# A routed FFN in which each half of a block takes its own expert

## The reference

```
# GNN, on the normalized x
h = layer_norm(x, gamma, beta)
conv = (adj @ h) @ W_rel + b_rel + h @ W_root
x = x0 + (x + relu(conv))            # x0 is the input, x its normalized form

# mixture of experts, on the normalized x
gate = x @ Wg.T + bg                 # 8 scores
topk_scores, topk_idx = top_k(gate, 2)
combine = softmax(topk_scores) placed at topk_idx
for e in range(8):
    h = relu(x @ W1[e].T + b1[e])    # 128 -> 512
    y = h @ W2[e].T + b2[e]          # 512 -> 128
    out = out + combine[e] * y
x = x + out
```

## Time and profile before

| what | us |
|---|---|
| median of 3 runs (479.68 to 481.05) | 480.88 |
| the profiled execution, its own time | 481.32 |
| its span, first to last instruction | 479.5 |
| PE matmuls busy | 393.0 (82%) |
| DVE busy | 315.6 (66%) |
| ACT busy | 271.5 (57%) |
| POOL busy | 249.9 (52%) |
| PE's share of the chain that ended last | 57% |

### The profile page before, as it was taken

The page is one execution under the profiler, slowest core; times in us unless marked ns, Lnnn a source line. Parts: engine busy times, 40 slices in busy tenths (PEclk is TensorE's granted clock), DMA queues, the critical chain, the costliest instruction groups (busy, mean ns, idle before and its releaser), DMA issues.

```text
span 479.5 us, 13216 instructions
## 1 busy us (share of the span) xinstructions
PE 393.0 (82%) x4371; PEld 350.2 (73%) x4371; DVE 315.6 (66%) x1055; ACT 271.5 (57%) x572; POOL 249.9 (52%) x263
## 2 busy tenths in 40 slices
PE   2888878789998679889867999999999999999000
PEld 2873735579997568889856988889999999998000
DVE  4875764685679497756898557765478545588511
ACT  1787583557885547786634686555555555554000
POOL 3002720177710377774007777777777750777770
PEclk9998785999999799999999999999999999999755
DMA  8991740164234234633436537647567857554520
GB/s 274 389 413 69 277 98 12 40 149 112 74 83 100 68 98 109 155 94 80 66 79 172 138 102 139 142 112 162 145 153 178 202 133 121 135 156 140 175 71 33
DMA packets 100721, 65.30 MB, mean 136 GB/s; under 512 B 66866, under 2 KB 92466, under 8 KB 100020
## 3 DMA queue, kind: packets, MB, share of 16 engines
q1 hardware_dynamic: 66292, 34.68, 27.4%
q0 software_dynamic: 8192, 16.79, 12.2%
q10 hardware_dynamic: 26176, 12.98, 11.1%
HBM read 19.58 MB, written 31.85 MB: 107 GB/s over the span
## 4 chain that ended last, share of the span: by engine, by line
PE 57%; DVE 22%; ACT 7%; issue 6%; DMA 3%; POOL 3%; ACTq 0%; SPq 0%; DVEq 0%; POOLq 0%
PE PY L951 7%; PE PY L946 7%; PE PY L947 7%; PE PH L927 6%; PE PH L929 6%; PE PH L928 6%; DVE HL L521 5%; POOL YG L307 3%; PE PY L938 2%; DVE STI L361 2%; PE PB L848 2%; PE PA L856 2%; PE PA L857 2%; ACT N L670 2%; DVE STO L407 1%
## 5 line engine op out<-in xcount | busy, mean ns | idle before, releaser
L294 POOL DMA_INDIRECT rows<-XHL,IDX x128 | 124.2, 970 | 136.0 <-DVE IDX L503 97.9
L521 DVE SCALAR_TENSOR_TENSOR HL<-PH,HH 128x512 f16<-128x512 f32 x198 | 129.9, 689 | 63.6 <-ACT HH L727 61.0
L307 POOL DMA_INDIRECT YG<-yrows,IDX x128 | 121.5, 949 | 81.7 <-DMA yrows<-YB 43.6
L727 ACT ACTIVATE HH<-PH 128x512 f16<-128x512 f32 x198 | 115.4, 594 | 29.4 <-PE PH L929 24.1
L947 PE MATMUL PY<-W2H,HL 128*128 x792 | 131.8, 220 | 0.0
L946 PE MATMUL PY<-W2H,HH 128*128 x792 | 131.8, 220 | 0.0
L927 PE MATMUL PH<-XT,W1H 128*128 128x256 f16 x396 | 108.1, 273 | 2.7 <-DVE HL L521 1.7
L951 PE MATMUL PY<-W2L,HH 128*128 x792 | 109.5, 220 | 0.0
L929 PE MATMUL PH<-XT,W1L 128*128 128x256 f16 x396 | 108.0, 273 | 0.0
L928 PE MATMUL PH<-XT,W1H 128*128 128x256 f16 x396 | 107.9, 273 | 0.0
L735 ACT ACTIVATE YB<-PY 128x256 f32<-128x256 f32 x99 | 37.9, 383 | 97.4 <-PE PY L951 92.3
(11 more groups left out here) (192 smaller groups left out, 504.8 us busy)
## 6 DMA issues: line engine op xcount, KB each, us to landing
yrows<-YB ACTq DMA_DIRECT2D x47, 256.0 KB
rows<-XT SPq DMA_DIRECT2D x2, 3072.0 KB, 16.3
YG<-in_w SPq DMA_DIRECT2D x2, 2048.0 KB, 11.3
out<-X SPq DMA_DIRECT2D x16, 256.0 KB
X<-in_x SPq DMA_DIRECT2D x3, 1024.0 KB, 5.5
ADJ<-in_adj SPq DMA_DIRECT2D x32, 64.0 KB
rows<-XHL,IDX POOLq DMA_INDIRECT x128
YG<-yrows,IDX POOLq DMA_INDIRECT x128, 2.5
```

Source lines behind the costliest of these rows:

```text
L294: nc.gpsimd.indirect_dma_start(rows[g % 2], bass.IndirectOffsetOnAxis(ap=IDX[:, col:col + 1], axis=0), XHL[:, src:src + 2 * P].bitcast(F32 ...
L307: nc.gpsimd.indirect_dma_start(YG[g % 2][:, dst:dst + P], None, yrows[g], bass.IndirectOffsetOnAxis(ap=IDX[:, col:col + 1], axis=0)).then_ ...
L521: nc.vector.scalar_tensor_tensor(HL[:, at:at + 2 * BW], PH[p % 2 * 2 + h][:, :], 0.0, HH[:, at:at + 2 * BW], ALU.max, ALU.subtract).then_i ...
L727: nc.scalar.activation(HH[:, at:at + 2 * BW], PH[p % 2 * 2 + h][:, :], ACT.Relu).then_inc((hia_made, hib_made)[h], 1)
```

## The change

The padding of the table goes to whole parts of 128 rows in place of 256. Two parts that follow one another form a block, and each has its own expert. A group then needs at most 2s + 7 parts, which is s + 4 blocks: 12, 20, 20, 20 and 12, in all 84.

- `expert(p)` becomes `experts(p)` and loads two registers.
- `hidden(p)` gets a loop over the two parts t: 24 matmuls of 128 columns, with the weights' address taken from the part's register, in place of 12 of 256 columns.
- `output(p)` works off the parts one after the other: each has its b2 matmul of 128 columns and 12 of the second layer. In all 26 matmuls of 128 columns in place of 24 and one of 256.
- `route_slots` pads to 128, `route_blocks` and the constants `K_FIRST` have 2 x NB[g] entries.
- The tables START, STATS, ROUTE and COMBINE have new block numbers.

```
-NB = [s + E - 1 for s in GS]
+NB = [(2 * s + E) // 2 for s in GS]
...
-START = {6: 5, 7: 7, 8: 9, 9: 11, 10: 17, 11: 20, 12: 23, 13: 26, 14: 39, 15: 43}
-STATS = {2: 1, 3: 12, 4: 35}
-ROUTE = {2: 16, 3: 32, 4: 49}
-COMBINE = {0: 30, 1: 32, 2: 66, 3: 68, 4: 70, 5: 72, 6: 90, 7: 92, 8: 94, 9: 96}
+START = {6: 4, 7: 6, 8: 8, 9: 10, 10: 14, 11: 17, 12: 20, 13: 23, 14: 34, 15: 38}
+STATS = {2: 0, 3: 9, 4: 30}
+ROUTE = {2: 15, 3: 29, 4: 44}
+COMBINE = {0: 31, 1: 33, 2: 54, 3: 56, 4: 59, 5: 61, 6: 75, 7: 77, 8: 79, 9: 81}
...
-                once(nc.vector.tensor_scalar(CNI[:, :], CNT[:, :], float(BW - 1), None, ALU.add))
+                once(nc.vector.tensor_scalar(CNI[:, :], CNT[:, :], float(P - 1), None, ALU.add))
...
-                once(nc.vector.tensor_scalar(PADI[:, :], CNI[:, :], 8, 8, ALU.logical_shift_right, ALU.logical_shift_left))
+                once(nc.vector.tensor_scalar(PADI[:, :], CNI[:, :], 7, 7, ALU.logical_shift_right, ALU.logical_shift_left))
...
-                m, b = GS[g], NB[g]
+                m, b = GS[g], 2 * NB[g]
...
-            def expert(p):
-                return nc.values_load(BEI[0:1, p:p + 1], engines=(mybir.EngineType.PE,), min_val=0, max_val=(E - 1) * P,
+            def experts(p):
+                return [nc.values_load(BEI[0:1, i:i + 1], engines=(mybir.EngineType.PE,), min_val=0, max_val=(E - 1) * P,
...
+                        for i in (2 * p, 2 * p + 1)]
...
+                    for t in range(2):
+                        hi, lo = XT[:, at + t * P:at + (t + 1) * P], XT[:, lo_at + t * P:lo_at + (t + 1) * P]
+                        for c in (2 * h, 2 * h + 1):
+                            o = PH[p % 2 * 2 + h][:, c % 2 * BW + t * P:c % 2 * BW + (t + 1) * P]
+                            wh = W1H[:, bass.ds(es[t] * C + c * P, P)]
+                            wl = W1L[:, bass.ds(es[t] * C + c * P, P)]
+                            nc.tensor.matmul(o, wh, hi, start=True, stop=False)
+                            nc.tensor.matmul(o, wh, lo, start=False, stop=False)
+                            last = nc.tensor.matmul(o, wl, hi, start=False, stop=True)
...
+                for t in range(2):
+                    o = PY[:, t * P:(t + 1) * P]
+                    nc.tensor.matmul(o, KH[:, H_B2M:H_B2M + P], B2[:, bass.ds(es[t], P)], start=True, stop=False)
+                    for c in range(C):
                         at = (p % 2 * C + c) * BW + t * P
...
+                        wh = W2H[:, bass.ds(es[t] * C + c * P, P)]
+                        wl = W2L[:, bass.ds(es[t] * C + c * P, P)]
+                        nc.tensor.matmul(o, HH[:, at:at + P], wh, start=False, stop=False)
+                        nc.tensor.matmul(o, HL[:, at:at + P], wh, start=False, stop=False)
+                        last = nc.tensor.matmul(o, HH[:, at:at + P], wl, start=False, stop=c == C - 1)
```

More of the change, by code:

```diff
@@ L77, in sem @@
             return ctx.enter_context(nc.semaphore(name))
-        rows = [nc.dram_tensor(f"rows{b}", [BW * (NBM + 1), P], F32, kind="Internal").ap() for b in range(2)]
+        rows = [nc.dram_tensor(f"rows{b}", [BW * NBM, P], F32, kind="Internal").ap() for b in range(2)]
         yrows = [nc.dram_tensor(f"yrows{g}", [BW * NB[g], P], F32, kind="Internal").ap() for g in range(G)]
@@ L130, in build @@
         B2F, BT = HL[:, :].bitcast(F32), HH[:, 0:E * P]
-        ZW = 2 * (NBM + 1) * P // 4
+        ZW = 2 * NBM * P // 4
         ZERO = XT[:, 0:2 * ZW].bitcast(F32)
@@ L908, in four_rest, with hidden @@
                     weight_rest(c)
-            def expert(p):
-                return nc.values_load(BEI[0:1, p:p + 1], engines=(mybir.EngineType.PE,), min_val=0, max_val=(E - 1) * P,
-                                      skip_runtime_bounds_check_because="the count of ends at or under a block is at most seven")
-            def hidden(p, e):
+            def experts(p):
+                return [nc.values_load(BEI[0:1, i:i + 1], engines=(mybir.EngineType.PE,), min_val=0, max_val=(E - 1) * P,
+                                       skip_runtime_bounds_check_because="the count of ends at or under a part is at most seven")
+                        for i in (2 * p, 2 * p + 1)]
+            def hidden(p, es):
                 ch = CB[p]
                 at = ch % XR * 2 * CW + (p - CH[ch][1]) * BW
-                hi, lo = XT[:, at:at + BW], XT[:, at + CH[ch][2] * BW:at + (CH[ch][2] + 1) * BW]
+                lo_at = at + CH[ch][2] * BW
                 if p == CH[ch][1]:
@@ L922, in hidden, with output @@
                         pe.wait_ge((loa_made, lob_made)[h], p - 1)
-                    for c in (2 * h, 2 * h + 1):
-                        o = PH[p % 2 * 2 + h][:, c % 2 * BW:(c % 2 + 1) * BW]
-                        wh = W1H[:, bass.ds(e * C + c * P, P)]
-                        wl = W1L[:, bass.ds(e * C + c * P, P)]
-                        nc.tensor.matmul(o, wh, hi, start=True, stop=False)
-                        nc.tensor.matmul(o, wh, lo, start=False, stop=False)
-                        last = nc.tensor.matmul(o, wl, hi, start=False, stop=True)
+                    for t in range(2):
[7 more added lines that the diff above has]
+                            last = nc.tensor.matmul(o, wl, hi, start=False, stop=True)
                     last.then_inc((ha_done, hb_done)[h], 1)
-            def output(p, e):
+            def output(p, es):
                 pe.wait_ge(loa_made, p + 1)
@@ L1014, in _ @@
                     pe.wait_ge(experts_made, P0.index(p) + 1)
-                e = expert(p)
+                es = experts(p)
                 if p == 1:
                     pe.wait_ge(wlo_made, 16)
-                hidden(p, e)
+                hidden(p, es)
                 for g, at in ROUTE.items():
@@ L1033, in _ @@
                     output(p - 1, before)
-                before = e
+                before = es
                 for n, at in START.items():
```

26 lines of the change are left out of this document (6 added, 20 removed).

## The result

| what | us |
|---|---|
| changed kernel, median of 4 runs (570.95 to 573.03) | 571.25 |
| kernel before, measured beside it, median of 4 (479.68 to 481.05) | 480.61 |
| ratio, 95% interval | 1.190 (1.187 to 1.193) |
| forecast (range) | 536 (508 to 572) |
| changed kernel, its profiled execution / span | 570.95 / 569.1 |

Slower by 90.6 us, where 55 were forecast: the direction is right, and the time lies 1 us inside the upper end of the range, 35 us above the forecast.

What follows compares the result with a forecast made beforehand. PE's matmul columns bound the kernel; after the change its sequencer would: 84 x 4.8 from 85.0 us gives 488, waits as instructions 493, data waits 499, matmuls and tail 534.5 of span, so 536 us; range 508 to 572.

Steps and rivals of the forecast that it cites:

- Bound of the kernel before: PE in the pure stage: matmul columns set 2.76 us per block, hiding the sequencer's 2.48 us with 0.28 to spare.
- Two experts per block, 4.8 us: PE's sequencer: doubled loads and register instructions need 4.8 us per block, 2.0 more than the columns, and become the bound.
- Second TENSOR_LOAD 0.36: PE's second expert load per block: taken as 0.36 us, bounds 0.11 (515 us in all) and 0.5 (548).
- Tables: START, STATS, ROUTE, COMBINE: new block numbers only move this work among blocks; slow blocks cover POOL's scatter and gather.
- Waits for data, 6 us: PE's waits for HL, MK and N: 24.5 us before, shrinking to 5, or 6 with a route_slots stall.
- Tail 35.0: From the last YB copy's start to the span's end: 36.0 us before, less 1.1 of waiting for gather 3.
- B: PE's clock falls through idling in every block: 610 us if held throughout, 570 in half the time; chance 0.12.
- C: PE's register instructions hide, the array bounds again; under about 3.5 us a block POOL bounds, 455 us; chance 0.06.
- D: No change: sequencer costs come out at 4.1 us per block instead of 4.8, loads overlapped, waits nothing; chance 0.02.

Runs made afterwards that it cites:

- halved columns alone: Kernel before, each 256-column matmul of the hidden part split in two of 128 with the same weight address: 768.02 us beside 761.2.
- second register: Kernel before, the block's expert loaded into two registers, second half's output addresses computed from the second, same matmuls: 823.26 us beside 761.2.
- joint load: Changed kernel with adjacency matrices of starts 8 and 9 issued sooner, plus one TENSOR_LOAD filling both registers: 827.23 us against 836.59 without the one load.
- the kernel without register work: Changed kernel with earlier matrices and weight addresses fixed at build, no TENSOR_LOAD or register instruction: 456.28 us beside 481.81 for the kernel before.
- the wide W2: Changed kernel, earlier matrices, one load for both registers, W2's high and low parts side by side for 256-column output matmuls: 797.4 us, 1.040 of kernel before.
- the two runs above: Kernel with W2's parts side by side, 797.4 us beside 767.36; the same with the register load one phase sooner, 794.66 us beside 767.18.

## Why the prediction was right, and where it was off

**Bound of the kernel before: right.** The sequencer's 2.48 us lay hidden under 2.76 us of columns with little to spare. One load and the output part's new addresses were enough to lift it over (4.05 us), and halved columns alone were not (2.79).

**Two experts per block, 4.8 us: right in mechanism and in each price, low by 0.29 us.** This is the main miss, 24 of 35 us. The term at fault is the sum 0.72 + 1.88 + 0.24 + 1.81 + 0.16: it adds the regular distances and takes their sum for the period. About every 32nd instruction of PE is late by 0.02 to 0.16 us. In the kernel before such a delay only uses up slack that the array covers, and a period of 2.76 us of columns shows none of it; when the sequencer is the bound, each one counts. The kernels that it bounded had nearly the same on top: 0.29 (changed), 0.26 (second register, of which 0.1 are longer loads), 0.26 (joint load: 4.95 against 4.69). The larger delays coincide with the packets of PE's instruction queue; the cause of the small ones is open.

**Second TENSOR_LOAD 0.36: right** (0.36 behind each). The rows put the second word of one load at 0.23 us and a load of one word at 0.30. The figure of the Trainium skill that the prediction cited, some 200 ns per register, fits the former and not the latter.

**Tables: wrong.** "They only move this work among blocks" left out the queue that the matrices' load shares with the row loads. The place in the code is named in the change (START 8), but the load's place in SP's queue follows from chunks, and the group's border moved under it from chunk 8 to chunk 6. I had read POOL's scatter to end before block 12 needs it and had not asked what else stands behind that wait on SP. It cost 6.8 us.

**Waits for data, 6 us: nearly right,** about 4 us of HL, MK and T, apart from the matrices. The quads' matmuls were put at nothing, since they were to fit into PE's idle time. Some steps took 6.8 to 7.0 us in place of 5.09 with a quad's work in them, and the mixed stage came out 3 us over its sum.

**Tail 35.0: right** (35.3), and POOL had time to spare, as forecast: it waited 110.2 us for yrows ahead of gathers.

**Rivals.** B (the clock falls): out, 1.00 in the late blocks, at 86% busy. Behind the wait for the matrices the clock did fall, from 140.7 to 147.5 us. C (the register instructions hide): out as a forecast, but what it said of POOL as the next bound is borne out by the kernel without register work (455 us, and 456.28 measured). D: out.

**The arithmetic.** Two sums are a little off as written: 499 + 0.3 + 35.0 is 534.3, not 534.5, and rival C's 85 + 84 x 4.1 + 11 + 35.3 + 1.4 is 477, so the change would break even at 4.13 us a block, not 4.1. Neither moves the forecast. That the measured 571.25 still lies in the range of 508 to 572 is luck in part: the range went up that far to take in half of B, not for the delays or the late load.

**A version that beats both** was not found. Without registers the change is worth 25 us (456.28 against 481.81); with the wide W2 the sequencer still needs 3.9 us a block by its sum against 2.8 of columns. In the two runs above it stays 4% over the kernel before. On a chip of the first kind it was not run; 571.25 - 6.8 - 84 x (5.09 - 4.28) is an estimate of 496 us for its best form, over 480.6 as well.

## What to carry to other kernels

A matmul with a register in its address costs PE's sequencer 0.11 to 0.12 us, a register load 0.36 (0.30 of them busy), in the traces here, and it doesn't matter how many columns they serve: so before a tile is cut smaller to waste less, add up what the sequencer does per tile and compare it with the columns. If that sum comes out on top, leave room for delays that the present bound hides (6% here). And when the number of blocks per group changes, look at each in-order queue for loads that now stand behind the wait of another group.

## What the hardware showed beyond that

**Standstills of TensorE on some chips.** On three chips the kernel before took 761 to 767 us in place of 481, and the changed one 835 in place of 571. In the changed kernel ten steps between blocks took over 12 us there, 312.8 us together, 262 more than 10 regular ones, nearly all of the 264 us between the two chips; the late blocks between them ran at 5.09 us. They lie where POOL issues its scatters and gathers, and that these cause them is not shown. 30 us of the changed kernel on such a chip and on one of the first kind, with POOL doing the same:

```profile
570.00:600.00 30.00, 4.84 (x34) 2.92 (x35) 1.83 (x7) 0.38 (x1) 22.70 (x24) 0.58 0.21 53
```

```profile
380.00:410.00 30.00, 25.64 (x294) 19.58 (x292) 14.86 (x36) 9.41 (x18) 22.63 (x25) 1.00 0.46 106
```

34 matmuls against 294. In order of time, on the chip with standstills:

```profile
576.96 0.27 PE L932 MATMUL PH<-XT,W1L 128*128 128x128 f16 x1 [1.85 <-issue]
577.02 0.31 PE L930 MATMUL PH<-XT,W1H 128*128 128x128 f16 x1
579.09 0.26 PE L931 MATMUL PH<-XT,W1H 128*128 128x128 f16 x1 [1.76 <-issue]
579.15 0.31 PE L932 MATMUL PH<-XT,W1L 128*128 128x128 f16 x1
580.52 0.27 PE L930 MATMUL PH<-XT,W1H 128*128 128x128 f16 x1 [1.06 <-issue]
```

One or two matmuls, then 1.1 to 1.9 us in which PE waits for nothing that the profile names, also between L930 and L931, which share an address, so it isn't the register work. Why some chips do this is open. Here a kernel's time on one chip said little about its time on another, while distances between undisturbed blocks still compared (5.09 on both).

**A register load can get longer.** A TENSOR_LOAD of two words took up to 1.16 us in place of 0.53 when it began 1.1 to 1.3 us after SP had begun to issue a transposing DMA. One of a single word did the same: in the kernel before with a second register, nine loads that began 1.5 to 1.6 us after such an issue took 0.39 to 0.64 us in place of 0.30 (two more at that distance did not).
